# Two-stage attention in a vision tower: two score banks, four maxima banks, reciprocals moved, slots evened out, query tiles in two halves

## The chip, the cores and the metric

The kernel runs on one core of one Trainium2 chip. The metric is the device time of one execution in microseconds (us), as the median of several runs. The core's engines are TensorE (PE, matmuls; PEld is its loading of stationary weights), VectorE (DVE), ScalarE (ACT), GpSimd (POOL) and SyncE (SP, here the queue that starts DMA transfers). Each engine works through its own instruction stream in order, and streams meet only at semaphores. Matmuls write to PSUM, which has eight banks of 512 float32 columns on each of 128 partitions.

## The reference, cut to what matters

The input is 4 images of 56 x 56 positions with 256 channels. A window attention (windows of 4 x 4) runs first, then a layer norm, an attention over all 3136 positions of an image, and a feed-forward block that is added for half of the positions. All is in float32. The change touches the second attention alone:

```python
qkv = (x @ qkv_w + qkv_b).reshape(Bw, Nw, 3, nh, dh)      # Bw = 4, Nw = 3136, nh = 8, dh = 32
q, k, v = (qkv[:, :, 0], qkv[:, :, 1], qkv[:, :, 2])
attn = jnp.einsum('bnhd,bmhd->bhnm', q * scale, k)
bias = jnp.transpose(rpb_table[rel_idx], (2, 0, 1))        # rel_idx = n - m + Nw - 1
attn = jax.nn.softmax(attn + bias[None], axis=-1)
out = jnp.einsum('bhnm,bmhd->bnhd', attn, v).reshape(Bw, Nw, Cd)
return out @ proj_w + proj_b
```

The table has 127 rows, so that the bias differs from a constant in one corner of the 3136 x 3136 scores only. The softmax subtracts each query's maximum over all keys before it takes exponentials.

## The kernel before, in words

`full_attention` (L755 to L1238) works in 8 phases, one for each image and each group of 4 heads. A phase has 7 halves (the code's word for a step), each for 448 queries: 56 halves in all. In a half the kernel computes, for the 4 heads, scores of 25 key tiles (64 keys, then 24 times 128) against the 448 queries, with keys on the partitions. That makes 100 score matmuls (`score`, L1016). Operands are split in a high and a low part that lie stacked in 96 rows, and a 97th row of the queries holds the negated maximum of each query, so that the score comes out of the matmul already shifted.

Each score goes to a PSUM bank of its own. ScalarE takes its exponential to `prob` (L1164), and this frees the bank: score i waits for the exponential that last used its bank (`bank_before`, L857 and L1023). There are three such banks (`SB`).

The maxima of the next half must be known before its scores. They need the same products once more with queries on the partitions: for a block of 128 queries, a head and a chunk of 448 keys, one matmul (`fill`, L1059, L1091) and one reduction by VectorE (`take`, L1188). A phase has 25 blocks x 4 heads x 7 chunks = 700 of these, and 14 "turns", in which TensorE transposes the collected maxima of two heads (L1070), VectorE copies them (L1183), and SP sends them to the 97th row of the queries (L917). A maximum's matmul waits for the reduction three entries earlier, since there are three banks for maxima (`MB`, L1065). The two sums, `ps_o` (outputs) and `ps_d` (denominators), take the last two banks.

`max_entries` (L725) writes the list of 714 entries and cuts it into seven slots, one for each half. Half h works on the entries of the slot of half h+1. The list follows the query blocks (4, 3, 4, 3, 4, 3, 4 of them belong to the seven query tiles); `SPILLS` says how many entries of the next tile's first block a slot takes as well, and `TURN_AFTER` how many entries behind its last maximum a turn stands. The slots before have 114, 92, 108, 92, 108, 92 and 108 entries.

TensorE's order in a half is written out by hand (L1111): score, then a maximum (so many that the slot ends with the half), and after scores 4, 12, 20, ... 100 a "burst" (L1098). A burst holds the matmuls of one or two tiles of `prob` with the values (`weigh`, L1035) and sometimes those for a denominator (`total`, L1047): 8 short matmuls each. The work between two bursts, 8 scores with their maxima, is called a stretch below. GpSimd adds the exponentials of three tiles at a time for the denominators (L997).

VectorE's order (L1211) is the slot's reductions, with the copy of the outputs before entry 4, and the 8 reciprocals of the previous half's denominators (L1206) before entries 25, 31, 37, ... (`FIRST_RECIP`, `RECIP_STEP`).

SP loads the 640 query columns of the half after next, for four heads at once, in three DMAs (L898) once the last score of the half before is out (L927). The first matmul that reads them waits for all three (L1083). The first block of a tile is read from a copy that is already there.

Of the kernel before, what the change touches and what calls it, by code (L numbers as in the profile page):

```python
# [25 lines left out]
CH = 448  # L26
# [690 lines left out]
GROUP_BLOCKS = [range(-(-7 * s // 2), -(-7 * (s + 1) // 2)) for s in range(PER_IMAGE)]  # L717
TILE_BLOCK = [7 * s // 2 for s in range(PER_IMAGE)]
MAX_EACH = HG * PER_IMAGE
SPILLS = [10, 16, 10, 16, 10, 16, 10]  # L720
TURN_AFTER = 4
SUM_TILES = [(1, 2, 3, 4)] + [(t, t + 1, t + 2) for t in range(5, 23, 3)] + [(23, 24)]


# [30 lines left out]
def full_attention(nc, d):  # L755

    with ExitStack() as ctx:
# [20 lines left out]
        shift_rows = [sb(f"shift_rows{p}", [8, BLK], F32R) for p in range(2)]  # L778
        den = sb("den3", [128, CH])
        out = [sb(f"out{i}", [128, CH]) for i in range(2)]  # L780
        SB = 3
        MB = 3
        ps_s = ps("ps_s3", [128, SB, 512])
        ps_m = ps("ps_m", [128, MB, 512])
        ps_o = ps("ps_o", [128, 512])
# [4 lines left out]
        id_zero, id_set, idr_set, ones_set, rows_set, tops_set = (  # L790
            sem("id_zero3"), sem("id_set3"), sem("idr_set"), sem("ones_set3"), sem("rows_set"), sem("tops_set"))
        k_in = [[sem(f"k_in{u}_{j}") for j in range(HG)] for u in range(2)]
        v_in, q_in = [sem(f"v_in{u}") for u in range(2)], [sem(f"q_in{u}") for u in range(2)]
        corner_in, ahead_in = sem("corner_in3"), sem("ahead_in")
        shift_in = [sem(f"shift_in{p}") for p in range(2)]
        o_kept, den_kept, recip_done, out_ready = sem("o_kept3"), sem("den_kept"), sem("recip_done"), sem("out_ready")
# [8 lines left out]
        ROUND = G * PER_IMAGE  # L805
        entries, slots = max_entries()
        ENTRIES = len(entries)
        assert ENTRIES % MB == 0
        ADDS = [len(tiles) - 1 for tiles in SUM_TILES]
        ADDS_HALF = sum(ADDS)  # L810
        start_counts(nc, sems, {tile_used: BEHIND})
# [55 lines left out]
        def entry_of_turn(s, p):  # L867
            return entries.index(("turn", s, p))

        def added(t):  # L870


            n = 0
            for tiles, adds in zip(SUM_TILES, ADDS):
                if t in tiles:
                    return n + max(1, tiles.index(t))
                n += adds

        @block.sync
        def _(sp):  # L880
# [13 lines left out]
            def load_queries(x):  # L894
                at = BLK * TILE_BLOCK[x.s]
                w = min(AHEAD, N - at)
                for row, part in ((0, 0), (DH, 0), (2 * DH, 1)):
                    sp.dma_start(queries[x.v][row:row + DH, :, 0:w].bitcast(F32),  # L898
                                 d.q[x.g, part, :, bass.ds(x.b * N + at, w)].rearrange("(j d) n -> d j n", j=HG)
                                 ).then_inc(q_in[x.v], 16)  # L900

            def load_ahead(x):

# [109 lines left out]
        def _(pe):  # L1013
# [45 lines left out]
            def fill(y, e, next_phase):  # L1059


                kind, group, *what = entries[e]
                p = y.p + next_phase
                if not (isinstance(p, int) and p == 0 and e < MB):
                    pe.wait_ge(m_used, ONE + ENTRIES * p + e - MB + 1)  # L1065
                if kind == "turn":
                    pair, = what
                    pe.wait_ge(shift_ready, ONE + 2 * PER_IMAGE * p + 2 * group + pair + 1)
                    base = TILE_BLOCK[group]
                    nc.tensor.transpose(ps_m[0:8, e % MB, 0:BLK],  # L1070
                                        shift[:, pair, base:base + 4, :].rearrange("q b j -> q (b j)"),
                                        ident[:, :]).then_inc(m_ready, 1)
                    return
                r, j, c = what
                u, v = (y.u + next_phase) % 2, (y.v + group + PER_IMAGE * next_phase - y.s) % 2
                very_first = isinstance(p, int) and p == 0 and group == 0
                ahead = r == GROUP_BLOCKS[group][0] and not very_first
                if group == 0 and r == 0 and c == 0:
                    pe.wait_ge(k_in[u][j], ONE + 48 * (y.b + int(next_phase and y.g == 1) + 1))
                    if j == 0 and not very_first:  # L1080
                        pe.wait_ge(ahead_in, ONE + 48 * p)
                if j == 0 and c == 0 and r == (0 if very_first else GROUP_BLOCKS[group][1]):
                    pe.wait_ge(q_in[v], ONE + 24 * (y.h - y.v) + 48)  # L1083
                tile = queries[1 - v if ahead else v]
                at = 4 * BLK if ahead else BLK * (r - TILE_BLOCK[group])
                rows = min(BLK, N - BLK * r)
                corner = r == 0 and c == PER_IMAGE - 1
                if corner and j == 0:
                    pe.wait_ge(corner_in, ONE + 32 * (p + 1))
                o = ps_m[0:rows, e % MB, :]  # L1090
                mm = nc.tensor.matmul(o[:, 0:CH], tile[0:STACK, j, at:at + rows], keys[u][0:STACK, j, c * CH:(c + 1) * CH],  # L1091
                                      start=True, stop=not corner, skip_group_check=corner)
                if corner:
                    mm = nc.tensor.matmul(o[:, CH - BLK:CH], corner_hi[:, j, :], ident_r[:, :],
                                          start=False, stop=True, skip_group_check=True)
                mm.then_inc(m_ready, 1)
# [75 lines left out]
        @block.vector  # L1172
        def _(dve):
            def take(y, e, next_phase):


                kind, group, *what = entries[e]
                p = y.p + next_phase
                dve.wait_ge(m_ready, ONE + ENTRIES * p + e + 1)
                if kind == "turn":  # L1180
                    pair, = what
                    dve.wait_ge(shift_in[pair], ONE + 32 * y.h)
                    nc.vector.tensor_copy(shift_rows[pair][:, :], ps_m[0:8, e % MB, 0:BLK]).then_inc(m_used, 1)  # L1183
                    return
                r, j, c = what
                blocks = GROUP_BLOCKS[group]
                rows = min(BLK, N - BLK * r)
                nc.vector.tensor_reduce(tops[0:rows, j, r - blocks[0], c:c + 1], ps_m[0:rows, e % MB, 0:CH],  # L1188
                                        AX.X, ALU.max).then_inc(m_used, 1)
                if r == blocks[-1] and j % 2 == 1 and c == PER_IMAGE - 1:  # L1190
                    pair = slice(j - 1, j + 1)
                    dve.wait_ge(m_used, ONE + ENTRIES * p + e + 1)
                    nc.vector.tensor_reduce(shift[:, j // 2, blocks[0]:blocks[-1] + 1, :].rearrange("q b j -> q j b"),
                                            tops[:, pair, 0:len(blocks), :],
                                            AX.X, ALU.max, negate=True).then_inc(shift_ready, 1)

            def keep_out(h, v):
                dve.wait_ge(tile_used, ONE + BEHIND + KT * (h + 1))
                dve.wait_ge(out_out[v], ONE + 8 * (h - v))
                nc.vector.tensor_copy(out[v][:, :], ps_o[:, 0:CH]).then_inc(o_kept, 1)  # L1200

            def recip(h, piece):
                w = CH // RECIPS
                if piece == 0:
                    dve.wait_ge(den_kept, ONE + h + 1)
                nc.vector.reciprocal(den[:, piece * w:(piece + 1) * w],  # L1206
                                     den[:, piece * w:(piece + 1) * w]).then_inc(recip_done, 1)

            FIRST_RECIP, RECIP_STEP, KEEP_AT = 24, 6, 4

            def half(x):  # L1211

                y = after(x)
                slot = [(e, n) for e, n in slots[y.s] if not (n and last_phase(y))] if x.has_next else []
                for at in range(max(len(slot), FIRST_RECIP + RECIP_STEP * RECIPS)):
                    if at == KEEP_AT * int(x.has_next) and x.has_before:
                        keep_out(x.h - 1, 1 - x.v)
                    if at < len(slot):
                        take(y, *slot[at])
                    piece, off = divmod(at - FIRST_RECIP, RECIP_STEP)  # L1220
                    if off == 0 and 0 <= piece < RECIPS and x.has_before:
                        recip(x.h - 1, piece)

            nc.vector.memset(tops[:, :, :, :], 0.0).then_inc(tops_set, 1)
            nc.vector.memset(shift[:, :, :, :], 0.0).then_inc(tops_set, 1)
            nc.vector.memset(ones[0:FIRST, 0, :], 1.0).then_inc(ones_set, 1)
            nc.vector.memset(ones[FIRST:128, 0, :], 0.0).then_inc(ones_set, 1)
            for u in range(2):
                nc.vector.memset(values[u][FIRST:128, 0, :], 0.0).then_inc(ones_set, 1)
            nc.vector.memset(prob[FIRST:128, 0, :, :], 0.0).then_inc(ones_set, 1)  # L1230
            dve.wait_ge(tops_set, ONE + 2)
            for e in range(slots[0][-1][0] + 1):
                take(Half(FIRST_ROUND, 0), e, 0)
            halves(dve, half)
            end = HALVES - 1
            keep_out(end, end % 2)
            for piece in range(RECIPS):
                recip(end, piece)  # L1238
# [491 lines left out]
```

## Time and profile before

| what | us |
|---|---|
| median of 3 runs (7252.97 to 7258.94) | 7256.23 |
| the profiled execution, its own time | 7257.0 |
| its span, first to last instruction | 7255.3 |
| PE busy | 6363.7 (88%) |
| DVE busy | 4829.3 (67%) |
| POOL busy | 4190.9 (58%) |
| ACT busy | 3313.5 (46%) |

The full attention takes the stretch from about 1545 to 5978 us of the span, in which PE's digit is 9 in nearly every slice. A busy matmul row is not a matmul at full speed: rows overlap, and a row that started late is as long as one that did not. So the stage is read from the distance between starts, not from busy time.

### The profile page before, as it was taken

The page shows a single profiled execution, that of the slowest core. Times are in us where ns is not written, and L with a number is a line of the kernel's source. Part 1 is how long each engine was busy: PE and PEld are TensorE (multiplying, and loading weights), DVE is VectorE, ACT ScalarE, POOL GpSimd, SP SyncE. Part 2 cuts the span into 40 slices and gives each one's busy share as a digit, 9 for nine tenths or more (in the row PEclk, how much of TensorE's full clock was granted, in tenths as well). Part 3 has the DMA queues.
Part 4 walks back from the last instruction along what each step waited for, and adds up shares of the span by engine and source line. Part 5 has one row for each costly group of instructions (what it writes and reads, how often), then busy time and mean ns, then how long its engine had stood idle before and what let it go on. Part 6 is the DMA issues. An engine that isn't in the chain of part 4 may idle for free. (4 is left out here: it accounts for less than half of the span.)

```text
span 7255.3 us, 126990 instructions
## 1 busy us (share of the span) xinstructions
PE 6363.7 (88%) x39184; PEld 3694.7 (51%) x39184; DVE 4829.3 (67%) x9450; ACT 3313.5 (46%) x6693; POOL 4190.9 (58%) x1309
## 2 busy tenths in 40 slices
PE   3777677789999999999999999999999994529999
PEld 2666555445555555555545555555555543316666
DVE  2666533377777777777777777777777747877661
ACT  1444311136656655656655656656656550002222
POOL 0222222258888888878878878878878884400000
PEclk9999899979999999999999999999999997769999
DMA  1111244431011001001101101111100003331110
GB/s 41 42 42 40 56 158 160 163 71 28 23 29 37 23 21 44 23 21 34 33 21 31 36 21 31 32 26 31 30 19 16 14 9 112 104 38 43 43 36 28
DMA packets 215237, 329.08 MB, mean 45 GB/s; under 512 B 50338, under 2 KB 176946, under 8 KB 211250
## 3 DMA queue, kind: packets, MB, share of 16 engines
q1 hardware_dynamic: 212106, 320.55, 16.5%
q8 instruction: 254, 4.16, 0.2%
q10 hardware_dynamic: 2664, 2.62, 0.2%
q14 instruction: 213, 1.74, 0.1%
HBM read 191.84 MB, written 130.88 MB: 44 GB/s over the span
## 5 line engine op out<-in xcount | busy, mean ns | idle before, releaser
L1188 DVE TENSOR_REDUCE tops<-ps_m 128x1 f32<-128x448 f32 (+1 forms) x5600 | 3074.7, 611 | 1159.7 <-PE ps_m L1091 1142.8
L1164 ACT ACTIVATE prob<-ps_s 128x448 f32<-128x448 f32 (+1 forms) x5600 | 2649.9, 556 | 1870.6 <-PE ps_s L1027 1840.6
L1091 PE MATMUL ps_m<-keys,queries 96*128 96x448 f32 (+1 forms) x5600 | 2289.2, 416 | 89.9 <-DVE tops L1188 46.1
L997 POOL TENSOR_TENSOR tile_sum<-prob 128x1792 f32<-128x1792 f32 x448 | 1803.6, 4026 | 784.8 <-ACT prob L1164 784.7
L1027 PE MATMUL ps_s<-queries,keys 97*128 97x448 f32 (+1 forms) x5600 | 2133.5, 388 | 14.4 <-ACT prob L1164 7.7
L997 POOL TENSOR_TENSOR tile_sum<-tile_sum,prob 128x1792 f32<-128x1792 f32 x448 | 1804.3, 4027 | 63.5 <-ACT prob L1164 36.2
L1091 PEld LDWEIGHTS ps_m<-keys,queries 96*128 96x128 f32 (+1 forms) x5600 | 1054.9, 188 | 728.7 <-DVE tops L1188 614.1
L1027 PEld LDWEIGHTS ps_s<-queries,keys 97*128 97x128 f32 (+1 forms) x5600 | 1041.2, 187 | 712.1 <-issue 536.9
L1043 PE MATMUL ps_o<-prob,values 128*32 128x448 f32 x11200 | 1209.1, 548 | 0.0
L1043 PEld LDWEIGHTS ps_o<-prob,values 128*32 128x32 f32 x11200 | 295.8, 109 | 519.9 <-ACT prob L1164 263.7
L255 POOL TENSOR_TENSOR logit<-logit,top 112x896 f32<-112x896 f32 x112 | 188.6, 1684 | 560.9 <-DVE top L372 560.9
L1560 PE MATMUL ps_y<-w_down,hT 128*112 128x256 f32 x1792 | 396.5, 382 | 108.5 <-DVE y L1627 86.7
L1594 DVE TENSOR_SCALAR_CACHE_REDUCE hits<-gate_row,own 112x112 bf16<-112x112 f32 (+13 forms) x328 | 418.1, 1324 | 19.6 <-DMA gate_row<-gate_rows 19.5
L1055 PE MATMUL ps_d<-tile_sum,ones 128*32 128x448 f32 x3584 | 421.7, 542 | 3.1 <-POOL tile_sum L997 3.0
L1560 PEld LDWEIGHTS ps_y<-w_down,hT 128*112 128x112 f32 x1792 | 316.6, 178 | 197.0 <-DVE y L1627 87.4
L279 PE MATMUL ps_q<-xT,w_qkv 128*128 128x224 f32 x896 | 214.0, 373 | 203.3 <-DMA xT<-in_x 104.6
L1552 PE MATMUL ps_h<-xnT,w_up 128*128 x896 | 343.2, 541 | 52.8 <-DMA b_down<-in_b_down 52.8
L1376 PE MATMUL ps_h<-w_proj,aT 128*112 128x256 f32 x448 | 160.8, 536 | 140.4 <-DVE h L1417 115.6
L1552 PEld LDWEIGHTS ps_h<-xnT,w_up 128*128 128x128 f32 x896 | 170.9, 191 | 212.0 <-issue 210.3
L1577 ACT ACT_TABLE_LOAD x28 | 35.9, 1283 | 526.9 <-PE ps_y L1560 474.8
L279 PEld LDWEIGHTS ps_q<-xT,w_qkv 128*128 128x128 f32 x896 | 159.5, 193 | 229.5 <-ACT qk L420 118.5
L702 ACT ACTIVATE full<-ps_q,bias_col 128x448 f32<-128x448 f32 x112 | 68.1, 633 | 455.9 <-POOL lo L568 356.9
(122 smaller groups left out, 4450.7 us busy)
## 6 DMA issues: line engine op xcount, KB each, us to landing
queries<-q_parts SPq DMA_DIRECT2D x144, 320.0 KB, 4.8
keys<-k_parts SPq DMA_DIRECT2D x96, 392.0 KB, 8.4
xT<-in_x SPq DMA_DIRECT2D x56, 224.0 KB, 2.5
window_out<-oT SPq DMA_DIRECT2D x56, 224.0 KB, 2.0
aT<-window_out SPq DMA_DIRECT2D x56, 224.0 KB, 3.8
hidden<-h SPq DMA_DIRECT2D x28, 448.0 KB, 4.5
q_parts<-hi SPq DMA_DIRECT2D x56, 224.0 KB, 1.9
q_parts<-lo SPq DMA_DIRECT2D x56, 224.0 KB, 2.0
```

Source lines behind the costliest of these rows:

```text
L255: nc.gpsimd.tensor_tensor(logit[p][:, :, :], logit[p][:, :, :], top[p][:, :].unsqueeze(2).broadcast_to([GROUP, NH, GROUP]), ALU.subtract). ...
L279: mm = nc.tensor.matmul(ps_q[:, job % 2, 0:UNIT], w[:, c, job * 128:(job + 1) * 128], xT[u][:, c, :], start=(c == 0), stop=(c == CT - 1))
L997: nc.gpsimd.tensor_tensor(tile_sum[k % 2][:, :, :], left, prob[:, t % SLOTS, :, :], ALU.add).then_inc(summed, 1)
L1027: mm = nc.tensor.matmul(o[:, 0:CH], keys[x.u][:, j, at:at + k], queries[x.v][:, j, own:own + CH], start=True, stop=not last, skip_group_ch ...
L1043: mm = nc.tensor.matmul(ps_o[j * DH:(j + 1) * DH, 0:CH], values[x.u][:, t, j * DH:(j + 1) * DH], prob[:, t % SLOTS, j, :], start=(t == 0), ...
L1055: mm = nc.tensor.matmul(ps_d[j * DH:(j + 1) * DH, 0:CH], ones[:, int(k > 0), :], moving, start=(k == 0), stop=(k == SUMS))
L1091: mm = nc.tensor.matmul(o[:, 0:CH], tile[0:STACK, j, at:at + rows], keys[u][0:STACK, j, c * CH:(c + 1) * CH], start=True, stop=not corner, ...
L1164: nc.scalar.activation(prob[0:k, t % SLOTS, j, :], ps_s[0:k, score_bank(x.hm, i), 0:CH], ACT.Exp).then_inc(exp_done, 1)
L1188: nc.vector.tensor_reduce(tops[0:rows, j, r - blocks[0], c:c + 1], ps_m[0:rows, e % MB, 0:CH], AX.X, ALU.max).then_inc(m_used, 1)
L1552: mm = nc.tensor.matmul(ps_h[:, t % 4, 0:CH], w_up[:, c, t * 128:(t + 1) * 128], xnT[:, m, c, :], start=(c == 0), stop=(c == CT - 1))
L1560: mm = nc.tensor.matmul(ps_y[0:QT, r, 0:C], hT[:, t, r * QT:(r + 1) * QT], w_down[:, t, :], start=(t == 0), stop=(t == HT - 1))
L1594: nc.vector.tensor_scalar(hits[:, i % 2, lo:hi], gates[:, lo:hi], mine, 0.0, op, ALU.add, accum_out=count[:, i, slot:slot + 1]).then_inc(c ...
```

## The change

- `SB` goes from 3 to 2, `MB` from 3 to 4.
- `SPILLS` and `TURN_AFTER` change. The slots become 108, 98, 102, 98, 102, 98 and 108 entries.
- The reciprocals stand before scores 28, 36, ... 84 of the half, by the entry that goes with them (`RECIP_SCORES`). Each of these points has a burst behind it.
- The queries are loaded for two heads at a time in six DMAs, with a semaphore for each pair.
- The bank of a maximum is counted on over the phases (`max_bank`), since 714 is no multiple of 4.

```diff
-SPILLS = [10, 16, 10, 16, 10, 16, 10]
-TURN_AFTER = 4
+SPILLS = [10, 22, 10, 22, 10, 22, 16]
+TURN_AFTER = 3
...
-        SB = 3
-        MB = 3
+        SB = 2
+        MB = 4
...
+        def max_bank(u, e):
+            return (e + u * ENTRIES) % MB
...
-                for row, part in ((0, 0), (DH, 0), (2 * DH, 1)):
-                    sp.dma_start(queries[x.v][row:row + DH, :, 0:w].bitcast(F32),
-                                 d.q[x.g, part, :, bass.ds(x.b * N + at, w)].rearrange("(j d) n -> d j n", j=HG)
-                                 ).then_inc(q_in[x.v], 16)
+                for pair in range(2):
+                    rows = slice(2 * pair * DH, 2 * (pair + 1) * DH)
+                    for row, part in ((0, 0), (DH, 0), (2 * DH, 1)):
+                        sp.dma_start(queries[x.v][row:row + DH, 2 * pair:2 * pair + 2, 0:w].bitcast(F32),
+                                     d.q[x.g, part, rows, bass.ds(x.b * N + at, w)].rearrange("(j d) n -> d j n", j=2)
+                                     ).then_inc(q_in[x.v][pair], 16)
...
-                if j == 0 and c == 0 and r == (0 if very_first else GROUP_BLOCKS[group][1]):
-                    pe.wait_ge(q_in[v], ONE + 24 * (y.h - y.v) + 48)
+                if j % 2 == 0 and c == 0 and r == (0 if very_first else GROUP_BLOCKS[group][1]):
+                    pe.wait_ge(q_in[v][j // 2], ONE + 24 * (y.h - y.v) + 48)
...
-            FIRST_RECIP, RECIP_STEP, KEEP_AT = 24, 6, 4
+            KEEP_AT = 4
+            RECIP_SCORES = [2 * HG * (k + 3) + HG for k in range(RECIPS)]
...
-                for at in range(max(len(slot), FIRST_RECIP + RECIP_STEP * RECIPS)):
+                pieces = [scores * len(slot) // TILES for scores in RECIP_SCORES]
+                for at in range(len(slot) + 1):
                     if at == KEEP_AT * int(x.has_next) and x.has_before:
                         keep_out(x.h - 1, 1 - x.v)
+                    for piece in range(RECIPS):
+                        if at == pieces[piece] and x.has_before:
+                            recip(x.h - 1, piece)
                     if at < len(slot):
                         take(y, *slot[at])
-                    piece, off = divmod(at - FIRST_RECIP, RECIP_STEP)
-                    if off == 0 and 0 <= piece < RECIPS and x.has_before:
-                        recip(x.h - 1, piece)
```

## Rows read from the trace of the kernel before

**Rows 1.** The page: busy time of the engines; TensorE's granted clock in 40 slices.
```profile
PE 6363.7 (88%) x39184; PEld 3694.7 (51%) x39184; DVE 4829.3 (67%) x9450; ACT 3313.5 (46%) x6693; POOL 4190.9 (58%) x1309
...
PEclk9999899979999999999999999999999997769999
```
**Rows 2.** Windows (length, PE and PEld busy, PEclk, DMA), scores alone: 55 halves, single ones.
```profile
1545.20:5906.80 4361.60, 2095.11 (x5500) 1023.46 (x5499) 1.00 0.12 28
...
2888.70:2970.20 81.50, 38.03 (x100) 18.70 (x100) 1.00 0.14 33
2970.20:3044.50 74.30, 37.85 (x100) 18.50 (x100) 1.00 0.16 37
...
5906.80:5978.00 71.20, 38.42 (x100) 17.50 (x100) 0.95 0.01 4
```
**Rows 3.** Waits of the stage: who waited for whom, us in total, times, longest.
```profile
PEld ps_m L1091 <- DVE tops L1188: 585.3, 2149, 0.7
...
PEld ps_s L1027 <- ACT prob L1164: 68.5, 256, 0.7
```
**Rows 4.** Windows of four stretches of 8 scores, maxima alone (L1091).
```profile
3015.82:3019.26 3.44, 2.51 (x7) 1.32 (x7) 1.00 0.00 0
2892.22:2896.14 3.92, 3.25 (x8) 1.50 (x8) 1.00 1.12 242
2898.55:2902.99 4.44, 3.69 (x9) 1.69 (x9) 1.00 0.00 0
2905.39:2910.19 4.80, 3.71 (x9) 1.69 (x9) 1.00 0.00 0
```
**Rows 5.** Windows, PE: bursts of 24 and 16 matmuls; the half's first 4 scores.
```profile
2903.00:2905.38 2.38, 2.38 (x25) 1.00 0.05 10
2910.20:2911.83 1.63, 1.63 (x17) 1.00 0.02 5
2888.80:2890.57 1.77, 1.77 (x12) 1.00 0.78 211
```
**Rows 6.** Timeline, PE (start, duration, work): a stretch's beginning, another stretch's end.
```profile
2892.22 0.47 PE L1027 MATMUL ps_s<-queries,keys 97*128 97x448 f32 x1
2892.53 0.37 PE L1091 MATMUL ps_m<-keys,queries 96*128 96x448 f32 x1
2892.74 0.37 PE L1027 MATMUL ps_s<-queries,keys 97*128 97x448 f32 x1
...
3018.97 0.36 PE L1091 MATMUL ps_m<-keys,queries 96*128 96x448 f32 x1
3019.27 0.58 PE L1043 MATMUL ps_o<-prob,values 128*32 128x448 f32 x4
```
**Rows 7.** Timeline, ACT and DVE: single work and work in a chain.
```profile
2892.73 0.54 ACT L1164 ACTIVATE prob<-ps_s 128x448 f32<-128x448 f32 x1 [1.64 <-PE ps_s L1027]
...
2892.94 0.62 DVE L1188 TENSOR_REDUCE tops<-ps_m 128x1 f32<-128x448 f32 x1 [0.61 <-PE ps_m L1091]
...
2899.26 4.34 DVE L1188 TENSOR_REDUCE tops<-ps_m 128x1 f32<-128x448 f32 x8 [1.98 <-PE ps_m L1091]
...
2908.25 0.49 DVE L1206 RECIPROCAL den<-den 128x56 f32<-128x56 f32 x1
```
**Rows 8.** Timeline, the last half (no maxima), one stretch: PE, then ACT.
```profile
5932.69 0.87 PE L1027 MATMUL ps_s<-queries,keys 97*128 97x448 f32 x3
5933.88 2.22 PE L1027 MATMUL ps_s<-queries,keys 97*128 97x448 f32 x5 [0.32 <-ACT prob L1164]
5936.02 0.58 PE L1043 MATMUL ps_o<-prob,values 128*32 128x448 f32 x4
...
5933.28 3.16 ACT L1164 ACTIVATE prob<-ps_s 128x448 f32<-128x448 f32 x7 [2.13 <-PE ps_s L1027]
```
**Rows 9.** DMAs of the queries (L898): to landing; their issues on SP's timeline.
```profile
DMA to landing us min/median/max: 3.2/4.8/7.3
...
2887.16 2.50 SPq L898 DMA_DIRECT2D queries<-q_parts  x3
```

More of the change, by code:

```diff
@@ L792, in full_attention @@
         k_in = [[sem(f"k_in{u}_{j}") for j in range(HG)] for u in range(2)]
-        v_in, q_in = [sem(f"v_in{u}") for u in range(2)], [sem(f"q_in{u}") for u in range(2)]
+        v_in = [sem(f"v_in{u}") for u in range(2)]
+        q_in = [[sem(f"q_in{v}_{pair}") for pair in range(2)] for v in range(2)]
         corner_in, ahead_in = sem("corner_in3"), sem("ahead_in")
@@ L807, in full_attention @@
         ENTRIES = len(entries)
-        assert ENTRIES % MB == 0
+        assert 2 * ENTRIES % MB == 0
         ADDS = [len(tiles) - 1 for tiles in SUM_TILES]
@@ L1062, in fill @@
                 kind, group, *what = entries[e]
-                p = y.p + next_phase
+                p, u = y.p + next_phase, (y.u + next_phase) % 2
                 if not (isinstance(p, int) and p == 0 and e < MB):
@@ L1069, in fill @@
                     base = TILE_BLOCK[group]
-                    nc.tensor.transpose(ps_m[0:8, e % MB, 0:BLK],
+                    nc.tensor.transpose(ps_m[0:8, max_bank(u, e), 0:BLK],
                                         shift[:, pair, base:base + 4, :].rearrange("q b j -> q (b j)"),
@@ L1074, in fill @@
                 r, j, c = what
-                u, v = (y.u + next_phase) % 2, (y.v + group + PER_IMAGE * next_phase - y.s) % 2
+                v = (y.v + group + PER_IMAGE * next_phase - y.s) % 2
                 very_first = isinstance(p, int) and p == 0 and group == 0
@@ L1089, in fill @@
                     pe.wait_ge(corner_in, ONE + 32 * (p + 1))
-                o = ps_m[0:rows, e % MB, :]
+                o = ps_m[0:rows, max_bank(u, e), :]
                 mm = nc.tensor.matmul(o[:, 0:CH], tile[0:STACK, j, at:at + rows], keys[u][0:STACK, j, c * CH:(c + 1) * CH],
@@ L1177, in take @@
                 kind, group, *what = entries[e]
-                p = y.p + next_phase
+                p, u = y.p + next_phase, (y.u + next_phase) % 2
                 dve.wait_ge(m_ready, ONE + ENTRIES * p + e + 1)
@@ L1182, in take @@
                     dve.wait_ge(shift_in[pair], ONE + 32 * y.h)
-                    nc.vector.tensor_copy(shift_rows[pair][:, :], ps_m[0:8, e % MB, 0:BLK]).then_inc(m_used, 1)
+                    nc.vector.tensor_copy(shift_rows[pair][:, :], ps_m[0:8, max_bank(u, e), 0:BLK]).then_inc(m_used, 1)
                     return
@@ L1187, in take @@
                 rows = min(BLK, N - BLK * r)
-                nc.vector.tensor_reduce(tops[0:rows, j, r - blocks[0], c:c + 1], ps_m[0:rows, e % MB, 0:CH],
+                nc.vector.tensor_reduce(tops[0:rows, j, r - blocks[0], c:c + 1], ps_m[0:rows, max_bank(u, e), 0:CH],
                                         AX.X, ALU.max).then_inc(m_used, 1)
```

## The prediction

> **What bounds the kernel now.** I read the page first. TensorE is busy 88% of the span, the others 46 to 67%, and the clock stands at 9 or more through the middle of the span [rows 1]. Busy PE rows overlap, so they don't tell whether TensorE works or waits. Next the windows: the 55 halves that have maxima beside them take 4361.6 us, 79.3 us each, and the last half 71.2 [rows 2]. Single halves differ: 74.3 where the slot has 92 entries and 81.5 for 108 [rows 2]: 0.45 us for an entry.
>
> The stretches show why. Between two bursts lie 8 scores; with 7 maxima this takes 3.45 us, with 8 3.93, with 9 4.45, and 4.80 where a reciprocal stands among them [rows 4]. TensorE needs 0.21 us for a matmul: the score after the maximum of 2892.53 starts at 2892.74 [rows 6]. Two are 0.42, yet the ninth maximum costs 0.52. VectorE sets that: 8 reductions in a chain take 4.34, the single one 0.62, so one follows another after (4.34 - 0.62) / 7 = 0.53 [rows 7]. With three banks, maxima beyond the first few wait for reductions: 2149 such waits against 256 for exponentials [rows 3]. Before each chain VectorE sat idle, 1.98 us before that one [rows 7], since a burst brings no maxima: it is late inside stretches only.
>
> **The round of a score bank.** This is the number the change turns on. From rows 6 to 8:
> - A score that had to wait takes 0.47 from its start to its end; one whose weights were loaded ahead 0.37. I count it from 0.10 after a late start, so that both are 0.37.
> - The exponential starts 0.04 after that end (2892.22 + 0.47, start 2892.73) and takes 0.54 by itself.
> - The next score of the bank: the exponential of 5933.28 ends at 5933.82, the fourth score (three banks) starts at 5933.88. That is 0.05 to 0.06, and 0.10 for the weights, 0.16 in all.
> The round is 0.37 + 0.04 + 0.54 + 0.16 = 1.11 us. Exponentials in a chain follow each other after (3.16 - 0.61) / 6 = 0.42 [rows 8], 0.61 being what a late one in a chain lasts. Three banks allow a score each 0.37, so ScalarE's own 0.42 limits; two allow one each 0.55.
>
> Check on what is known, three and three banks with 8 maxima, starts from the stretch's start: scores 0.10, 0.52, 0.94, then 1.35; maximum k is reduced from 0.72 + 0.53k and lasts 0.62, so maximum k+3 can start at 1.50 + 0.53k. Maximum 3 starts at 1.56 behind its score, maximum 4 at 2.03, maximum 7 at 3.62; 0.29 later comes the burst (3018.97 to 3019.27 [rows 6]): 3.91. The row says 3.92 [rows 4].
>
> **Two score banks, four for maxima.** The same with the change. Even scores: 0.10; the exponential runs 0.51 to 1.05; score 2 at 1.21, score 4 at 2.32, score 6 at 3.43. Odd ones: score 1 at 0.52, its exponential 0.93 to 1.47 (0.42 after the first); score 3 at 1.63, score 5 at 2.74, score 7 at 3.84. Maximum 7 at 4.05, burst at 4.34. Maximum k+4 needs reduction k: the fifth maximum could start at 1.50 and the eighth at 3.1, and TensorE comes to them at 2.5 and 4.05. So the waits for VectorE are gone, and the scores' own round is what is late next: 4.34 instead of 3.93. A ninth maximum is free behind an odd score (there is 0.2 of idle time before each even one) and costs 0.21 behind an even one. The first 4 scores of a half end at 1.63 + 0.21 + 0.29 = 2.13 instead of 1.77 [rows 5].
>
> **Even slots.** Today's entries cost more at the top than at the bottom; at three and three banks the even slots would give (weights 3 of 98, 2 of 102, 2 of 108) about 1 us a half. With two score banks nearly all stretches are 4.34, so evenness gives almost nothing: 98 entries 12 x 4.34, 102 0.2 more, and 108 about 1.0 more, since its 8 extras fall five times behind an even score.
>
> **Reciprocals.** Eight a half, 0.49 each [rows 7]. A stretch with one is 0.35 longer today (4.80 against 4.45 [rows 4]). Behind the last maximum of a stretch, VectorE ends at about 5.2 + 0.4 = 5.6 after the stretch's start; the burst hides it (4.34 + 1.64 is 6.0 [rows 5]). They cost nothing then. But this saving of up to 8 x 0.35 a half lies in the same VectorE waits that the banks removed, so it isn't added. GpSimd's multiplication waits for the last one, before score 84, and comes behind tile 21's exponential, score 88: covered by 2 us.
>
> **Queries in six DMAs.** Slots 2, 4 and 6 begin 22 entries into their first block, so 6 ahead are left instead of 12 before the new columns are needed. The seventh entry comes 1.64 (burst), 2.13, 1.64 and 1.7 after the last score, 7.1 us. SP issues three DMAs in 2.5 us, and each lands after 3.2 to 7.3, median 4.8 [rows 9]; half-size ones for the first pair should be nearer to 3.2, so about 6. I take no cost. Bounds: nothing, and at most 3 us in 24 halves, 70 us. SP's three added issues are 1.3 us of an idle queue; the keys behind them are needed halves later, and the row of maxima now starts an entry or more earlier.
>
> **Turns** come an entry earlier, each entry now being 0.55 instead of 0.42 to 0.53: VectorE has as long as before for the last reduction. No cost.
>
> **The sum.** Bursts of a half: 8 of 24 matmuls and 5 of 16, 8 x 2.39 + 5 x 1.64 = 27.3 [rows 5]. A new half with 98 entries is 27.3 + 2.1 + 12 x 4.34 = 81.5, with 102 81.8 (0.2 rounded up), with 108 82.6; the mean is 81.9. The halves before are 79.3, of which some 0.2 are loop ends and late DMAs that my stretches don't hold, so 82.1: +2.8, in 55 halves +154. The last half has no maxima: 12 stretches of 3.84 + 0.29 = 4.13 instead of 3.33 [rows 8], and 0.4, +10. In 14 halves, those outside the loop, the first exponential of a tile starts 0.12 instead of 0.04 after its score (5932.69 + 0.47, start 5933.28 [rows 8]); in the round of two banks this lies on the path, 14 x 12 x 0.08 = +14. Together +178. The profiled execution took 7257.0 (span 7255.3, 1.7 around it), 0.8 above the median: 7435 us. Inside this case the round may be 0.03 off, 3.5 rounds in each of 700 stretches: 70 us either way.
>
> **The pages.** The rows show that a bank is held for 0.54 by an exponential although ScalarE takes the next after 0.42. The Trainium skill (ScalarE: Activation LUTs, What ACT_TABLE_LOAD costs) has an activation with immediate operands at 186 ns + 0.833 ns an element, for 448 elements 0.56 us by itself, and about 93 ns less back to back. By it the round would be 0.02 longer and the stretch 0.06: an estimate of 7475 us. The trace agrees on the first and is lower.
>
> The Trainium skill (TensorE: Matmul & The Clock Gate, A second HAM failure mode) also says that cycling through PSUM banks can make the engine idle so often that its clock swings. That speaks against this change. In this trace the stage has the clock at 1.00, and 0.95 in the last half, where TensorE has least to do [rows 2]. I give this 0.04 of rival C's chance.
>
> **The rivals.**
> A. *The bank comes free earlier* than the exponential's recorded end: after 0.42. Then the round is 0.99, score 7 at 3.49, the burst at 3.98, a half 27.3 + 2.0 + 12 x 3.98 = 77.1, with extras and remainder 77.4: -105 and a few for the last half, 7155. For it: ScalarE does start the next after 0.42. Against it: the fourth score of rows 8 starts behind the end, not 0.12 before it. The view on consistent bubbles of the Trainium skill (Perfetto Trace Analysis, Optimization Strategy) would have the fourth bank of maxima pay in this way.
> B. *Faster, below that*: scores could keep the 3.45 of a stretch with 7 maxima. That half is 27.3 + 1.8 + 12 x 3.55 = 71.7, total 6850. Only if the score round doesn't matter at all; rows 8 speak against it.
> C. *Slower than forecast*: the first pair's queries land late (+70), or the clock falls to the last half's 0.95 (5% of the 69 us that matmuls stream in a half, +190): 7505 to 7625.
> D. *No change*: 0.2 a stretch too much in my round would be needed, no row shows it.
>
> **How the numbers follow.** Forecast 0.74, A 0.09, B 0.03, C 0.10, D 0.04. A measurement here can tell 0.2% (15 us) from no change: faster 0.13, same 0.04, slower 0.83. The range from 7340 to 7510 leaves out A, B and part of D below and part of C above, about 0.2; the forecast's own is 7365 to 7505.
>
> **What would show it.** Right: waits of scores for exponentials (256 now) in the thousands, those of maxima for reductions nearly gone, stretches at 4.3 to 4.4 whatever their maxima, halves at 81 to 83, all alike, and no reciprocal inside a stretch that TensorE waits for. Wrong: starts of scores i and i+2 less than 1.05 apart in a stretch (A), a wait of L1091 for `q_parts` or a clock under 0.98 (C).

## The result: 3.1% slower

The changed kernel takes 7482.8 us (median of 4 runs) against 7254.6 before, a ratio of 1.031 [1.030, 1.033]. The forecast was 7435 in a range of 7340 to 7510. The profiled execution took 7474.75, 217.75 more than the one of before; it was the shortest of the four, so the medians lie 10 us further apart (228).

Windows of the changed kernel, scores alone (now L1033): 55 halves, then two halves of the loop, one behind it, the last. They answer to [rows 2].
```profile
1544.50:6108.90 4564.40, 2357.39 (x5500) 1014.52 (x5499) 1.00 0.10 26
2204.90:2287.00 82.10, 42.83 (x100) 18.47 (x100) 1.00 0.15 38
2287.00:2368.80 81.80, 42.73 (x100) 18.38 (x100) 1.00 0.13 30
5098.20:5182.30 84.10, 42.90 (x100) 18.46 (x100) 1.00 0.15 37
6108.90:6195.20 86.30, 43.03 (x100) 18.07 (x100) 0.90 0.01 3
```
A half is now 4564.4 / 55 = 83.0 us instead of 79.3, and nearly the same whatever its slot: 39 of the 42 halves in the loop take 81.8 to 83.7, where the kernel before had 74.3 to 85.3. The whole difference lies here: the first score starts at 1544.6 (1545.2 before), the last at 6195.2 (5977.5).

Waits of the stage, and the duration of the scores (min/median/max in ns), which answer to [rows 3]:
```profile
PEld ps_s L1033 <- ACT prob L1170: 876.0, 2365, 1.0
...
L1033 PE MATMUL ps_s<-queries,keys x5600: 358/460/743, 1544.6 to 6195.2; 97*128 97x448 f32 x186, 97*64 97x448 f32 x8
...
  ACT prob L1170: 909.3, 2497
...
DVE tops L1194 <- PE ps_m L1097: 1199.5, 798, 5.3
```
Scores wait for exponentials 2365 times instead of 256, and the median score lasts 0.46: more than half of them started late. (The text on the profile before says that a row that started late is as long as one that did not. These rows say otherwise: 0.47 against 0.37 for a score.) Waits of maxima for reductions, 2149 before, are gone from the stage's list, and 108 are left in the first part where maxima run alone.

A stretch of the loop on PE, with the score and the maxima of it; then ACT. It answers to [rows 6, 7].
```profile
2304.51 0.47 PE L1033 MATMUL ps_s<-queries,keys 97*128 97x448 f32 x1
2304.82 0.37 PE L1097 MATMUL ps_m<-keys,queries 96*128 96x448 f32 x1
2305.03 0.37 PE L1033 MATMUL ps_s<-queries,keys 97*128 97x448 f32 x1
...
2305.61 0.47 PE L1033 MATMUL ps_s<-queries,keys 97*128 97x448 f32 x1
...
2306.12 0.39 PE L1033 MATMUL ps_s<-queries,keys 97*128 97x448 f32 x1
...
2306.72 0.47 PE L1033 MATMUL ps_s<-queries,keys 97*128 97x448 f32 x1
...
2307.82 0.47 PE L1033 MATMUL ps_s<-queries,keys 97*128 97x448 f32 x1
2308.13 0.37 PE L1097 MATMUL ps_m<-keys,queries 96*128 96x448 f32 x1
2308.34 0.39 PE L1033 MATMUL ps_s<-queries,keys 97*128 97x448 f32 x1
2308.57 0.37 PE L1097 MATMUL ps_m<-keys,queries 96*128 96x448 f32 x1
2308.87 0.58 PE L1049 MATMUL ps_o<-prob,values 128*32 128x448 f32 x4
...
2305.02 4.29 ACT L1170 ACTIVATE prob<-ps_s 128x448 f32<-128x448 f32 x8 [2.46 <-PE ps_s L1033]
```
Every even score is late (0.47), 1.10 to 1.11 behind the even one before it (2305.61, 2306.72, 2307.82): the round of a bank. From the start of the stretch the burst comes at 4.36. Over the whole loop, counted from the starts in the trace, the median stretch of 8 scores lasts 4.36 with 8 maxima and 4.54 with 9. And the reciprocal, on VectorE, behind the last reduction and under the burst, which covers the time to the next stretch (VectorE is done at 2310.10, 5.59 after the stretch's start; the forecast had 5.6):
```profile
2305.22 4.47 DVE L1194 TENSOR_REDUCE tops<-ps_m 128x1 f32<-128x448 f32 x8 [2.28 <-PE ps_m L1097]
2309.61 0.49 DVE L1212 RECIPROCAL den<-den 128x56 f32<-128x56 f32 x1
2311.23 1.16 DVE L1194 TENSOR_REDUCE tops<-ps_m 128x1 f32<-128x448 f32 x2 [1.13 <-PE ps_m L1097]
```

### The profile page after: what moved, and what is told of

The parts are those of the page before. It is cut to its first block and busy times, and to the rows that moved or that the text cites. A ratio compares the mean times of both kernels' runs of the same rounds, so it can differ in the third digit from the quotient of the medians.

```text
span 7473.0 us, 127411 instructions
## 1 busy us (share of the span) xinstructions
PE 6585.4 (88%) x39184; PEld 3570.7 (48%) x39184; DVE 4937.1 (66%) x9450; ACT 3423.4 (46%) x6693; POOL 4191.7 (56%) x1309
## 3 DMA queue, kind: packets, MB, share of 16 engines
q1 hardware_dynamic: 214794, 320.56, 15.6%
q14 instruction: 224, 1.84, 0.1%
## 5 line engine op out<-in xcount | busy, mean ns | idle before, releaser
L1194 DVE TENSOR_REDUCE tops<-ps_m 128x1 f32<-128x448 f32 (+1 forms) x5600 | 3146.1, 618 | 1243.9 <-PE ps_m L1097 1209.5
L1170 ACT ACTIVATE prob<-ps_s 128x448 f32<-128x448 f32 (+1 forms) x5600 | 2759.3, 542 | 1977.7 <-PE ps_s L1033 1743.3
L1033 PE MATMUL ps_s<-queries,keys 97*128 97x448 f32 (+1 forms) x5600 | 2400.9, 431 | 71.0 <-ACT prob L1170 33.3
L1097 PE MATMUL ps_m<-keys,queries 96*128 96x448 f32 (+1 forms) x5600 | 2056.8, 376 | 35.6 <-DMA keys<-k_parts 20.2
L1033 PEld LDWEIGHTS ps_s<-queries,keys 97*128 97x128 f32 (+1 forms) x5600 | 1033.0, 185 | 1666.4 <-ACT prob L1170 876.0
```

Of the source, the lines that this page charges most:

```text
L1033: mm = nc.tensor.matmul(o[:, 0:CH], keys[x.u][:, j, at:at + k], queries[x.v][:, j, own:own + CH], start=True, stop=not last, skip_group_ch ...
L1170: nc.scalar.activation(prob[0:k, t % SLOTS, j, :], ps_s[0:k, score_bank(x.hm, i), 0:CH], ACT.Exp).then_inc(exp_done, 1)
```

## The experiments

R is the theory that the round of a score bank (matmul, exponential, release) sets the stretches. Medians are in us; ratios are to the kernel before on the same chip, with 95% intervals. The kernel before took 7254.6 beside the changed kernel, 7264.5 beside e1, e2, e3 and e8, 7262.0 beside e4, e5, e6 and e9, and 7264.5 beside e10. So a difference between a run and the changed kernel is good to some 10 us.

### e1: three and three banks, all else of the change kept
```diff
-        SB = 2
-        MB = 4
+        SB = 3
+        MB = 3
```


> The changed kernel with three score banks and three maxima banks again; the even slots, the moved reciprocals and the split query loads stay. Theory R (the round of a score bank sets the stretches of the changed kernel, all other parts help or are free): stretches with 8 maxima return to 3.93 us, those with 9 to 4.45, none is at 4.80; a half averages 78 us instead of 82.6, and the time is 7190 us, below the kernel before (7255). Rival Q (part of the loss comes from the slots, the query loads in six parts or the reciprocals): the time stays above 7255.

7181.8, ratio 0.989 [0.987, 0.991]: 1.1% faster than before. A stretch with 8 maxima, maxima alone:
```profile
2292.41:2296.33 3.92, 3.26 (x8) 1.50 (x8) 1.00 0.00 0
```
So the banks cost 7483 - 7182 = 301 us (307 by the ratios), and the rest of the change is worth some 83 (7264.5 - 7181.8). Q falls.

### e2: the two and four banks alone
`SB` and `MB` as in the change, with `max_bank`; slots, reciprocals and loads as before.

> The kernel before with two score banks and four maxima banks, nothing else of the change. Theory R: all stretches 4.37 to 4.55 us whatever they hold, reciprocals inside a stretch cost nothing since four banks cover them, so the time is that of the changed kernel, 7470 to 7510 us. Rival Q: clearly less, about 7350, with the rest of the loss in the other parts. Rival V (the fourth maxima bank does not cover a reciprocal inside a stretch): over 7550.

7497.4, ratio 1.032 [1.031, 1.034], inside R's range. Two stretches with 9 maxima (maxima alone), and VectorE in the first:
```profile
2821.72:2826.08 4.36, 3.08 (x9) 1.71 (x9) 1.00 0.02 6
2828.47:2832.82 4.35, 3.06 (x9) 1.71 (x9) 1.00 0.00 0
...
2825.11 0.49 DVE L1210 RECIPROCAL den<-den 128x56 f32<-128x56 f32 x1
```
A reciprocal stands inside the stretch and costs nothing: 4.36, where the kernel before had 4.80 [rows 4]. V falls, and so does Q. Under two score banks the other parts, worth 83 us at three, are worth 15 by the medians and 9 by the ratios, which the intervals don't tell from nothing.

### e3: exponentials over half of the columns
This leaves work out: half of the probabilities is a constant, set once (the lines that set it are not shown).
```diff
-nc.scalar.activation(prob[0:k, t % SLOTS, j, :], ps_s[0:k, score_bank(x.hm, i), 0:CH],
+nc.scalar.activation(prob[0:k, t % SLOTS, j, 0:224], ps_s[0:k, score_bank(x.hm, i), 0:224],
```


> The changed kernel with each exponential over 224 of its 448 columns (the other half of the probabilities is a constant), so that a score bank is held for 0.36 instead of 0.54 us. Theory R: the round of a bank falls from 1.11 to 0.93, score 7 of a stretch starts at 3.30 instead of 3.84, a stretch lasts 3.80 to 3.85 instead of 4.37, and the time falls by 700 x 0.55 = 380 us to about 7100. Rival W (TensorE's own order or VectorE holds the stretch at 4.37): no change, 7480.

7093.9, ratio 0.977 [0.975, 0.978]. A stretch (maxima alone), its second and third even scores, and an exponential by itself:
```profile
2297.26:2301.04 3.78, 2.85 (x8) 1.52 (x8) 1.00 0.17 61
...
2298.20 0.45 PE L1033 MATMUL ps_s<-queries,keys 97*128 97x448 f32 x1
...
2299.11 0.46 PE L1033 MATMUL ps_s<-queries,keys 97*128 97x448 f32 x1
...
2297.78 0.36 ACT L1170 ACTIVATE prob<-ps_s 128x224 f32<-128x224 f32 x1 [2.64 <-PE ps_s L1033]
```
The exponential is 0.18 shorter, and the round (2298.20 to 2299.11) 0.91 instead of 1.11. TensorE's work, VectorE's and their order are those of the changed kernel, so it is the exponential's time that costs, and 389 us hang on it. W falls. By itself e3 also makes ScalarE's own pace faster; that this is not what counts is seen in e1, where a full exponential with a third bank gives 3.92.

### e8: two score banks, three for maxima, one unused


> The changed kernel with two score banks and only three maxima banks, one bank unused. Theory R: under the score round, maxima come to TensorE 0.55 us apart, more than VectorE's 0.53, and reciprocals lie under the bursts: the fourth bank is worth nothing, the time is that of the changed kernel within 15 us (7483). Rival V: the fourth bank still covers something at the turns or behind the reciprocals, and the time is 30 us or more above the changed kernel.

7492.2, ratio 1.031 [1.029, 1.033]; the changed kernel's is 1.031 [1.030, 1.033]. With two score banks the fourth bank for maxima is worth nothing that these runs can tell: 9 us by the medians, none by the ratios. 85 waits of maxima for reductions come back, 17.7 us in all. V falls.

e8 and e1 ran on the same chip and differ in one score bank alone (two or three, three maxima banks in both): 7492.2 and 7181.8. The third score bank by itself is worth 310 us.

### e4: four score banks, two for maxima


> The changed kernel with four score banks and two maxima banks, the mirror of the change. Theory R applied to VectorE: a maximum's bank is held for 0.37 + 0.04 + 0.62 + 0.16 = 1.19 us, two banks allow a maximum each 0.60, maximum 7 starts at 4.41 and the burst at 4.70 instead of 4.37; a ninth maximum costs 0.6 now. A half is about 87.5 instead of 82.6, the time 7700 to 7780 us. Rival (maxima fit into the gaps of the scores and two banks are enough for them): 7250 or less.

7768.1, ratio 1.070 [1.068, 1.071]. A stretch with 8 maxima (maxima alone), and the stage's largest wait of TensorE:
```profile
2337.61:2342.30 4.69, 3.47 (x8) 1.50 (x8) 1.00 0.00 0
...
PEld ps_m L1097 <- DVE tops L1194: 1327.6, 3940, 0.8
```
4.69 for an expected 4.70: the same count of a round holds for VectorE's bank.

### e5 and e6: slots alone; reciprocals and query loads alone
Both have three and three banks.

> The kernel before with the new slots alone (98 to 108 entries; three and three banks, reciprocals and query loads as before). With three banks an entry costs 0.45 to 0.6 us at every size, and a reciprocal costs more in a stretch of 8 maxima than in one of 7. Theory R: gain and loss meet, 7264 within 20 us. Rival E (evenness is what makes the three-bank version faster): 7200 or less. Rival Q (six ahead entries are too few for a load of four heads): waits of maxima for q_parts, 7290 or more.

> The kernel before with the reciprocals ahead of the bursts and the queries in six DMAs, slots and banks as before. Theory R: no stretch of 9 maxima at 4.80 any more, eight reciprocals a half at 0.2 to 0.35 each come off TensorE's path, 7264 - 56 x 1.6 = 7175 to 7200 us. Rival E: less than 20 us of gain, the rest being evenness.

Slots alone: 7270.7, ratio 1.001 [1.000, 1.002], no gain. It has a wait that the kernel before does not have:
```profile
PE ps_m L1095 <- DMA queries<-q_parts: 6.8, 10, 2.0
```
Ten waits of maxima for their queries, at most 2.0 us, 6.8 in all, too little for rival Q's 7290; the changed kernel, with its loads in six parts, has none. Rival E falls too. Reciprocals and loads alone: 7193.5, ratio 0.991 [0.989, 0.992], 68 us less than the 7262.0 of before. The two were not run apart, but the kernel before has no wait for `q_parts` that smaller loads could save, and stretches of 9 maxima fall from 4.80 to 4.45, so the 68 us are put down to the reciprocals. That leaves some 14 of e1's 83 us for the slots: alone they cost 9, on top of the moved reciprocals they gain a little.

### e9 and e10: a burst after every tile
```diff
-            for t in range(0, KT, 2):
-                i = HG * min(t + 2, KT) + 3
-                bursts[i % TILES] += [(weigh, k, i >= TILES) for k in range(t, min(t + 2, KT))]
+            for t in range(KT):
+                i = HG * (t + 1) + 3
+                bursts[i % TILES].append((weigh, t, i >= TILES))
```


> The changed kernel with three and three banks and a burst after every 4 scores (one tile of values each) instead of every 8. Banks are empty again after each burst, and three banks cover 4 maxima: the 4 scores at the start of a half take 1.78 us, against 3.93 for 8. A burst of 8 matmuls should cost 0.88 (0.094 a matmul and 0.13 for the change of work). Theory R: 25 x 1.78 + 272 x 0.094 + 25 x 0.13 = 73.4 and 0.8 for extras and turns, 74.2 a half instead of 77.5 in the three-bank version (7182): about 7000 us, the fastest. Rival P (GpSimd's sums, 65.5 us of work in each half, or ScalarE's chain become late): 7080 or more, with waits of L1061 or L1170 for sums. Rival S (a change of work costs more than 0.13): 7182 or above.

> The changed kernel (two score banks, four for maxima) with a burst after every 4 scores, the edit that took the three-bank version from 7182 to 7113 us. Theory R: with two banks the third and fourth score of a stretch wait for exponentials in short stretches too, 2.12 us for 4 scores, so two short stretches and the added change of work (2 x 2.12 + 0.25) are longer than one of 4.37: a half 82.3 against 81.9 by the same count, and the time is 7490 to 7515 us, no gain or a small loss against 7483. Rival F (splitting the bursts pays by itself, whatever the banks): about 7410.

e9 (three and three): 7113.0, ratio 0.979 [0.978, 0.981], the fastest that does all the work. e10 (two and four): 7513.8, ratio 1.034 [1.033, 1.036], no faster than the changed kernel. A stretch of 4 scores in each, maxima alone; for e9 also one of the tile of 64 keys and one with a fifth maximum, and its waits for GpSimd's sums:
```profile
2298.52:2300.35 1.83, 1.38 (x4) 0.76 (x4) 1.00 0.00 0
2307.48:2309.26 1.78, 1.38 (x4) 0.76 (x4) 1.00 0.90 230
2229.53:2231.84 2.31, 1.86 (x5) 0.94 (x5) 1.00 0.17 58
...
ACT prob L1170 <- POOL tile_sum L1003: 16.2, 11, 1.7
PEld ps_d L1061 <- POOL tile_sum L1003: 4.9, 2, 3.8
```
```profile
2305.50:2307.65 2.15, 1.41 (x4) 0.76 (x4) 1.00 0.00 0
```
In e10 the third score already waits. With three banks, the waits for VectorE hardly arise in 4 maxima: an edit that pays 69 us at three banks costs 31 at two by the medians, 22 by the ratios. e9 missed its 7000 by 113. Its stretches are 1.84, not 1.78: I had the 1.78 from the first 4 scores of a half [rows 5], which belong to the tile of 64 keys, whose weights load in 0.13 to 0.14 instead of 0.19. That is 24 x 0.06 x 56 = 81 us of the 113. A fifth maximum in a stretch costs 0.47 to 0.48, and a half has two on average, which uses up the 0.8 set down for extras and turns. How the other 32 us divide was not followed. The time does lie in P's range (7080 or more), but not for P's reason: the waits for sums are 21 us in all, and e1 has more of ScalarE's (37.0 us, 14 times). S falls: a burst of 8 takes 0.89 for 0.88.

## Why the prediction was right

- **The round.** 1.11 expected, 1.10 to 1.11 measured. The starts of the scores, counted from the stretch's start, were to be 0.52, 1.11 (1.21 less the 0.10 of a late start), 2.22 and 3.33 for scores 1, 2, 4 and 6; they are 0.52, 1.10, 2.21, 3.31, and the burst 4.36 for 4.34. e3 changed one part of the round and moved the stretch as counted; e4 did the same with VectorE's.
- **Maxima off the path.** Right, but not by the fourth bank: e8 has three and its ratio is the same. What frees them is that scores come 0.55 apart, slower than VectorE's 0.53.
- **Even slots, reciprocals.** "Evenness gives almost nothing" and reciprocals "cost nothing then" but add no saving: e2 against the changed kernel, 15 us at most. At three banks I expected about 1 us a half (56 us) of evenness. That was wrong: e5 shows none. By the medians of the loop's stretches, a reciprocal costs 0.34 in one of 8 maxima (4.27 against 3.93, in e5) and 0.14 in one of 7 (3.60 against 3.46, in the kernel before), and the even slots have more stretches of 8.
- **Queries.** No wait for `q_parts`. Half-size loads land after 2.1 to 5.3, median 3.2, for 3.2 to 7.3, median 4.8 [rows 9]:
```profile
DMA to landing us min/median/max: 2.1/3.2/5.3
```
- **The sum.** +178 forecast, +218 in the profiled executions. From score to score: the 42 halves of the loop +3.06 each for 2.8; the 12 behind it +5.26 for 3.8; the first half +10.9 for 3.8 (it had a slot of 92 and was the cheapest before, and I gave each half the mean); the last +15.6 for 11. Of the last half's 15.6, its bursts are 2.6: some of them last longer there (31.5 us of bursts instead of 28.9), under the lower clock named below.
- **The term that was mis-sized for a known reason** is "14 x 12 x 0.08 = +14". The late start of a tile's first exponential is in the trace of both kernels, but a stretch has two tiles, so it comes twice, and both times in the even scores' round. PE and ACT in a stretch behind the loop, its window (maxima alone), and what stands in ScalarE's stream just ahead of the two exponentials:
```profile
5200.12 0.47 PE L1033 MATMUL ps_s<-queries,keys 97*128 97x448 f32 x1
...
5202.42 0.47 PE L1033 MATMUL ps_s<-queries,keys 97*128 97x448 f32 x1
...
5200.72 0.54 ACT L1170 ACTIVATE prob<-ps_s 128x448 f32<-128x448 f32 x1 [2.54 <-PE ps_s L1033]
...
5203.01 0.98 ACT L1170 ACTIVATE prob<-ps_s 128x448 f32<-128x448 f32 x2 [0.21 <-PE ps_s L1033]
...
5200.12:5204.63 4.51, 2.86 (x8) 1.52 (x8) 1.00 0.00 0
...
L1169 ACTq EVENT_SEMAPHORE  x2: 38/38/38, 5200.6 to 5202.9; - x2
```
5200.12 + 0.47 to 5200.72 and 5202.42 + 0.47 to 5203.01 are 0.13 and 0.12, where the loop has 0.04 (2304.98 to 2305.02). The stretch is 4.51 instead of 4.36, 0.15 x 12 = 1.8 us a half, nearly all of the 2.0 between a half behind the loop and the same half in it (84.1 and 82.1). The doubled term is 13 of the 40 us that the sum is short; 11 are the loop's 42 x 0.26, 6 the first half's cheap slot, 2.6 the last half's bursts, and the rest was not followed.

  As for why such an exponential starts later: ScalarE's stream has 350 waits as instructions of their own (`EVENT_SEMAPHORE`, L1169), one for each tile of the 14 halves outside the loop, and the first exponentials there start 0.12 after their scores (median, none under 0.09). The loop has no such wait, and its 1050 first exponentials start 0.04 after their scores (median). The two go together, but no run took the wait away, so the cause stays open.
- **The clock.** 1.00 in the stage, as forecast; in the last half, where TensorE waits most, 0.90 for the 0.95 of before, which is in the 15.6 for 11 there.

The pages: the Trainium skill's figures (ScalarE: Activation LUTs, What ACT_TABLE_LOAD costs) put the exponential at 0.56 and gave an estimate of 7475; the rows have 0.54, and the profiled 7474.75, which this estimate met, was made up by the terms above, not by a longer exponential: that is luck. The Trainium skill (Perfetto Trace Analysis, Optimization Strategy) says of consistent bubbles that they can mean too little buffer space for the next tile. For the scores the runs agree: the third score bank is worth 310 us (e8 and e1). For the maxima they don't: with two score banks the fourth maxima bank pays nothing (e8).

## What to carry to other kernels

Before moving a bank from one consumer to another, write down each bank's round: matmul, start of the reader, the reader's whole recorded duration, release and weight load. Divided by the number of banks it is the least distance between two pieces of work; compare it with what the other engine in the same in-order stream allows. Here three score banks gave 0.37, so that ScalarE's own 0.42 was the limit, and two gave 0.55, more than VectorE's 0.53 that was to be cured. Where a consumer is late only at the end of a long stretch, shorter stretches (e9) or moving its other work under a burst (e6) cure it without a bank.

## Not expected

The count of a round held within 0.02 us for both readers and at both sizes of the exponential. The granted clock of the last half fell from 0.95 to 0.90 with two banks, with the same instructions and longer waits between them.
